# An attention and ternary-FFN layer on eight cores: weight thresholds one cut earlier, sums eight units ahead, the causal mask added on VectorE, and one query product for 129 rows

## The reference, cut to what matters

```python
# x: (2, 16384, 1024), 16 heads of 64, 4 sinks, window 512, FFN 1024 -> 4096 -> 1024
def attn(x):                       # x is the layer-normed input
    q, k, v = split_heads(x @ Wq), split_heads(x @ Wk), split_heads(x @ Wv)
    ctx = 4 sinks + last 512 positions of k and v          # t_ctx = 516
    logits = einsum(q, ctx_k) / 8
    logits = where(cols <= rows + (516 - t), logits, -inf) # so only the last
    w = softmax(logits); w = where(isnan(w), 0, w)         # 516 rows see anything
    return einsum(w, ctx_v) @ Wo
def bitlinear(x, W):
    scale = clip(mean(abs(W), axis=1), 1e-5)
    return x @ (clip(round(W / scale), -1, 1) * scale).T
def ffn(x):
    h = bitlinear(x, w_fc) + gate * (x @ v.T @ fast_b.T @ u.T)
    return bitlinear(relu(h) ** 2, w_proj)
x = x + layernorm(attn(layernorm(x)))
x = x + layernorm(ffn(layernorm(x)))
```

## Time and profile before

| | us |
|---|---|
| three runs | 1111.68 (median), 1111.23, 1113.1 |
| the profiled execution | 1114.61 |
| its span, slowest core (core 5) | 1113.0 |
| spans of the eight cores | 1104.3 to 1113.0 |
| PE busy | 1036.8 (93%) |
| DVE busy | 577.4 (52%) |
| ACT busy | 372.6 (33%) |

### The profile page before, as it was taken

How to read it: one execution, slowest core, us unless ns; L and a number is a source line. 1 busy time by engine, 2 the same in 40 slices (tenths; PEclk the granted TensorE clock), 3 DMA queues, 4 the chain that set the end, 5 groups by cost and what they waited for, 6 DMA issues and landing times.

```text
span 1113.0 us, 15478 instructions; the slowest of 8 cores (1104.3 to 1113.0 us)
## 1 busy us (share of the span) xinstructions
PE 1036.8 (93%) x5173; PEld 477.1 (43%) x5173; DVE 577.4 (52%) x905; ACT 372.6 (33%) x701; POOL 15.7 (1%) x33
## 2 busy tenths in 40 slices
PE   3788858977999999999999999999999999999997
PEld 1222335533454444444445444454444444444443
DVE  3878889676343553454434353454435544444333
ACT  4577798313431143112421044112421143014300
POOL 0000000000000000000000000000000000000000
PEclk9988967998999999999999999999999999999999
DMA  8999976474123511362043510572016310321011
GB/s 261 202 228 231 225 248 210 117 202 137 36 54 93 144 44 23 87 149 70 19 63 93 142 44 6 98 159 94 16 29 150 107 39 6 102 84 39 1 61 54
DMA packets 101489, 115.91 MB, mean 104 GB/s; under 512 B 77581, under 2 KB 77837, under 8 KB 101412
## 3 DMA queue, kind: packets, MB, share of 16 engines
q1 hardware_dynamic: 97444, 102.59, 34.6%
q0 software_dynamic: 3728, 12.25, 5.9%
q10 hardware_dynamic: 240, 0.07, 0.0%
HBM read 87.79 MB, written 17.31 MB: 94 GB/s over the span
## 4 chain that ended last, share of the span: by engine, by line
PE 86%; DVE 5%; issue 4%; DMA 2%; ACT 2%; DVEq 0%; ACTq 0%; SPq 0%; POOLq 0%
PE fcb L477 38%; PE pjp L491 36%; PE xp L491 1%; PE xp L531 1%; PE xp L628 1%; PE xp L590 1%; PE fcb L491 1%; DVE below L1196 1%; PE pjp L542 1%; DMA r<-v 1%; DVE below L1202 1%; DMA lrow<-ctx 1%; DMA xy<-wpj 1%; PE xp L670 0%; PE xp L613 0%
## 5 line engine op out<-in xcount | busy, mean ns | idle before, releaser
L477 PE MATMUL fcb<-xnT,Sfc 128*128 128x512 bf16 x2048 | 468.2, 388 | 4.8 <-DVE r L1144 4.7
L491 PE MATMUL pjp<-Spj,r 128*128 128x512 fp8e4 x1920 | 422.5, 380 | 0.0
L477 PEld LDWEIGHTS fcb<-xnT,Sfc 128*128 128x128 bf16 x2048 | 198.9, 99 | 257.6 <-issue 36.1
L491 PEld LDWEIGHTS pjp<-Spj,r 128*128 128x128 bf16 x1920 | 185.9, 98 | 223.9 <-issue 5.7
L1144 DVE TENSOR_TENSOR r<-fcb,rpp 128x512 bf16<-128x512 f32 x224 | 154.3, 691 | 236.2 <-ACT rpp L841 235.1
L841 ACT ACTIVATE rpp<-fcb,hsc 128x512 f32<-128x512 f32 x224 | 153.6, 687 | 238.2 <-PE fcb L477 237.5
L813 ACT ACTIVATE lv<-mv,cvecs 128x1 f32<-128x1 f32 x64 | 18.7, 293 | 304.4 <-DVE mv L1126 216.8
L1116 DVE TENSOR_TENSOR xy<-pjp,oscb 128x512 f32<-128x512 f32 x60 | 41.3, 688 | 151.1 <-PE pjp L491 151.1
L1121 DVE BATCH_NORM_STATS2 s<-xy 128x6 f32<-128x512 f32 x64 | 44.4, 694 | 9.1 <-DVE xy L1116 5.7
L1138 DVE TENSOR_TENSOR xy<-xy 128x1024 f32<-128x1024 f32 x32 | 39.1, 1223 | 4.7 <-DVE xy L1130 4.7
L542 PE MATMUL pjp<-identb,tern 128*128 128x128 bf16 x256 | 25.2, 257 | 15.3 <-DVE tern L1206 8.5
(11 more groups left out here) (138 smaller groups left out, 529.9 us busy)
## 6 DMA issues: line engine op xcount, KB each, us to landing
out<-xy SPq DMA_DIRECT2D x32, 512.0 KB, 2.9
xy<-x SPq DMA_DIRECT2D x31, 512.0 KB, 4.9
xs<-x SPq DMA_DIRECT2D x29, 512.0 KB, 4.9
xy<-wfc SPq DMA_DIRECT2D x16, 512.0 KB, 5.0
xy<-wpj SPq DMA_DIRECT2D x13, 512.0 KB, 5.2
stg<-wpj SPq DMA_DIRECT2D x11, 512.0 KB, 5.1
stg<-wfc SPq DMA_DIRECT2D x10, 512.0 KB, 5.3
xs<-wpj SPq DMA_DIRECT2D x8, 512.0 KB, 5.1
```

The costliest lines, as they stand in the source:

```text
L477: mm = te.matmul(fcb[n % 3][:, 0:TT], s_fc[:, dci * HF + hc * 128:dci * HF + hc * 128 + 128], xnT[:, dci * TT:(dci + 1) * TT], start=(dci ...
L491: mm = te.matmul(dst, r2[:, hc * TT + s * 128:hc * TT + s * 128 + 128], s_pj[:, hc * D + half * 512: hc * D + half * 512 + 512], start=(hc ...
```

## The change

- `AHEAD` is 8 instead of 7: ACT does the sum of unit n + 8 in step n, and one sum more before the loop.
- `group` of the fc units (but the first) stands ahead of `cut(n + 2)`, not behind it. `ut` moves from steps n % 4 == 1, ahead of `fc`, to steps n % 4 == 0, behind `fc`. `ut_copy` moves to the end of steps n % 4 == 0. The first such group keeps its place (n == 0 and n == 1).
- The mask has 516 columns, zero for the sinks, and is added by DVE: `Sm` = `xp` + `mask`; maximum and exponential read `Sm`. PE no longer multiplies it in.
- `queries` multiplies the 128 rows and the lone row at once, 129 columns.

```diff
--- before.py
+++ after.py
@@ -38,7 +38,7 @@
 NUNIT = NFU + NPU
 GRP = 4
 NSLOT = 9
-AHEAD = 7
+AHEAD = 8
 
 NG = 6
 GROWS = [128, 128, 128, 128, 128, 5]
@@ -69,7 +69,7 @@
     DI = lambda n, s: nc.dram_tensor(n, s, F32, kind="ExternalInput")
     t_x = DI("x", [TOK, D])
     t_ctx = DI("ctx", [CN, D])
-    t_mw = DI("mw", [128, WIN])
+    t_mw = DI("mw", [128, CTX])
     t_ms = DI("ms", [NH, SINKS])
     t_cvec = DI("cvec", [128, 8])
     t_id = DI("ident", [128, 128])
@@ -135,7 +135,8 @@
             QB = asb("QB", [128, DCN * NH], BF16)
             KS = asb("KS", [128, DCN * SINKS], BF16)
             VS = asb("VS", [SINKS, D], BF16)
-            mask = asb("mask", [128, WIN], BF16)
+            mask = asb("mask", [128, CTX], BF16)
+            Sm = asb("Sm", [128, CTX], F32)
             msB = asb("msB", [NH, SINKS], F32)
             OT = asb("OT", [128, DCN * NACT + 2], BF16)
             ast6 = asb("ast6", [128, 12], F32)
@@ -607,15 +608,14 @@
             def queries(q):
                 w = wt(3 * q + 1)
                 te.wait_ge(a_k, 2 * q + 2)
-                for lo, n, at in ((CA, 128, 0), (CB, 1, 256)):
-                    for kk in range(2):
-                        for dc in range(DCN):
-                            mm = te.matmul(
-                                xh[0][:, at + kk * n:at + kk * n + n],
-                                w[:, dc * 256 + kk * 128:
-                                  dc * 256 + kk * 128 + 128],
-                                ctxT3[:, dc, lo:lo + n],
-                                start=(dc == 0), stop=(dc == DCN - 1))
+                for kk in range(2):
+                    for dc in range(DCN):
+                        mm = te.matmul(
+                            xh[0][:, kk * NACT:kk * NACT + NACT],
+                            w[:, dc * 256 + kk * 128:
+                              dc * 256 + kk * 128 + 128],
+                            ctxT3[:, dc, CA:CA + NACT],
+                            start=(dc == 0), stop=(dc == DCN - 1))
                 mm.then_inc(p_q, 1)
 
             def values(q, k):
@@ -643,8 +643,6 @@
                 q, k = divmod(h, 4)
                 r = slice(64 * (h % 2), 64 * (h % 2) + 64)
                 te.wait_ge(a_q, q + 1)
-                if h == 0:
-                    te.wait_ge(d_msk, 32)
                 if k > 0:
                     te.wait_ge(a_e, h)
                 if k == 1:
@@ -652,10 +650,9 @@
                 if k == 2:
                     te.wait_ge(a_o, 2 * q + 1)
                 qa = QA[r, (k // 2) * 128:(k // 2) * 128 + 128]
-                te.matmul(xh[0], identb[:], mask[:], start=True, stop=False)
                 te.matmul(xh[0], qa, KT[r, (k // 2) * WIN:
                                         (k // 2) * WIN + WIN],
-                          start=False, stop=True)
+                          start=True, stop=True)
                 te.matmul(xh[1][:, 0:SINKS], qa,
                           KS[r, (h // 2) * 4:(h // 2) * 4 + 4],
                           start=True, stop=True).then_inc(p_s, 1)
@@ -761,12 +758,12 @@
             for n in range(NUNIT):
                 if n >= NFU:
                     unit(n)
-                if n % GRP == 1 and n + 3 < NFU:
-                    ut(n // GRP + 1)
                 if 2 <= n < HCN + 2:
                     fc(0, n - 2)
                 if n == 0:
                     low_rank(2)
+                if n == 1 or (n > 1 and n % GRP == 0 and n + 4 < NFU):
+                    ut(n // GRP + 1)
                 if n + 3 < NFU:
                     low_rank(n + 3)
                 if n > NFU and n % GRP == 3:
@@ -905,12 +902,15 @@
                 sc.wait_ge(p_q, q + 1)
                 if q == 0:
                     sc.wait_ge(v_zero, 1)
-                sc.activation(QA[:], xh[0][:, 0:256], AF.Copy)
+                sc.activation(QA[:].rearrange("p (k n) -> p k n", n=128),
+                              xh[0][:, 0:2 * NACT].rearrange(
+                                  "p (k n) -> p k n", n=NACT)[:, :, 0:128],
+                              AF.Copy)
                 for e in range(2):
                     r = slice(64 * e, 64 * e + 64)
                     at = 36 * q + e
                     cp = sc.activation(QB[r, at:at + 19:18],
-                                       xh[0][r, 256:258], AF.Copy)
+                                       xh[0][r, 128:2 * NACT:NACT], AF.Copy)
                 cp.then_inc(a_q, 1)
 
             def values(q, k):
@@ -926,7 +926,7 @@
                 sc.wait_ge(v_mx, h + 1)
                 if h > 0:
                     sc.wait_ge(d_pt, 16 * h)
-                sc.activation(Pb[:, 0:CTX], xp[:, 0:CTX], AF.Exp, scale=0.125,
+                sc.activation(Pb[:, 0:CTX], Sm[:], AF.Exp, scale=0.125,
                               bias=nmx[:, 1:2],
                               accum_out=nmx[:, 2:3]).then_inc(a_e, 1)
 
@@ -1023,18 +1023,21 @@
             turned(3)
             abssum(5)
             abssum(6)
+            abssum(7)
             for n in range(NUNIT):
                 if n + AHEAD < NUNIT:
                     abssum(n + AHEAD)
                 if n >= NFU:
                     evac(n)
-                if n % GRP == 1 and n + 3 < NFU:
-                    ut_copy(n // GRP + 1)
+                if n == 1:
+                    ut_copy(1)
                 if n == NFU + 15:
                     out_scale(0)
                 if 3 <= n < HCN + 3:
                     relu(0, n - 3)
                     square(n - 3)
+                if n > 1 and n % GRP == 0 and n + 4 < NFU:
+                    ut_copy(n // GRP + 1)
             out_scale(1)
             for j in range(NTILE):
                 i = NSUB * j
@@ -1232,8 +1235,12 @@
                                  ALU.mult).then_inc(v_lnr, 1)
 
             def scores(h):
+                if h == 0:
+                    ve.wait_ge(d_msk, 32)
                 ve.wait_ge(p_s, h + 1)
-                settled(ve.reduce_max(nmx[:, 0:1], xp[:, 0:CTX], axis=AX.X,
+                settled(ve.tensor_tensor(Sm[:], xp[:, 0:CTX], mask[:],
+                                         ALU.add))
+                settled(ve.reduce_max(nmx[:, 0:1], Sm[:], axis=AX.X,
                                       negate=True))
                 ve.tensor_scalar(nmx[:, 1:2], nmx[:, 0:1], 0.125, None,
                                  ALU.mult).then_inc(v_mx, 1)
@@ -1297,10 +1304,12 @@
             cut(0)
             cut(1)
             for n in range(NUNIT):
+                if n > 1 and n % GRP == 0 and n + 4 < NFU:
+                    group(n // GRP + 1)
                 if n + 2 < NUNIT:
                     cut(n + 2)
-                if n % GRP == 0 and n + 4 < NFU:
-                    group(n // GRP + 1)
+                if n == 0:
+                    group(1)
             for j in range(NTILE):
                 i = NSUB * j
                 more = j + 1 < NTILE
@@ -1383,7 +1392,9 @@
             [x[beta, T - WIN:T], act, one, x[beta, 0:SINKS]], axis=0))
         jw = np.arange(WIN)[None, :]
         rr = 128 * i + np.arange(128)[:, None]
-        m["mw"] = np.where(jw <= rr, 0.0, NEG).astype(np.float32)
+        m["mw"] = np.concatenate(
+            [np.where(jw <= rr, 0.0, NEG), np.zeros((128, SINKS))],
+            axis=1).astype(np.float32)
         cs = np.arange(SINKS)[None, :]
         m["ms"] = np.ascontiguousarray(np.broadcast_to(
             np.where(cs <= i, 0.0, NEG).astype(np.float32), (NH, SINKS)))
```

## The result

The changed kernel took **1105.54 us** (median of 4 runs, 1103.62 to 1106.7), the kernel before 1112.39 beside it (4 runs, 1111.23 to 1113.9). The ratio is 0.9936, 95% interval 0.9916 to 0.9956: 6.85 us less, where 10.3 were forecast. The profiled execution took 1105.06 us; its slowest core is core 2. Some executions of every kernel, changed or not, show a lower granted clock on part of the cores and take longer; all ratios here leave these out.

What follows compares the result with a forecast made beforehand. PE was taken as full in the tiles, a DVE-PE-ACT wait loop as limiting the fc units. Terms -9.7 + 2.0 + 1.2 - 3.5 - 1.5 + 1.2 = -10.3 us, from 1111.68 to 1101.4 us; range 1095 to 1108.5.

Steps and rivals of the forecast that it cites:

- parts 1 and 2: Fc units: thresholds first in the step remove a loop of waits, -9.7 us; loads landing late then cost +2.0.
- part 1: Fc units: thresholds one cut earlier leave no wait in the DVE-PE-ACT loop, 12.1 us a group, -9.7 us.
- the group that was to hide: Fc units: the second group of thresholds hides in DVE's wait ahead of unit 6, put at 0.7 us.
- part 3: Projection units: unit 47's copy on ACT waits behind a sum whose load is asked for later, +1.2 us, bounds 0 and 2.1.
- part 4: Attention: 16 mask matmuls leave PE, 0.216 us each, -3.5 us; 5.0 if the change of weights costs more.
- part 5: Attention queries: 16 matmuls a call instead of 32, four calls at 0.38 us, -1.5 us.
- part 6: Attention: mask add on DVE delays exponential, relus and squares, so PE waits at seven fc-stage scores, +1.2 us, bounds 0 and 5.6.
- the loads': Fc units: landings near 7 us keep the spacing nearly as before, 1107.5 us; chance 0.2.
- the clock's: Fc units: the granted clock still falls once a group, 0.5 us a group leaks through, 1104.4 us; chance 0.1.
- the slower one: Fc units: the turn's new place lowers the clock longer in every group, 15.01 us spacing, 1116.2 us; chance 0.04.
- The mask rival: Attention: the mask add stalls PE at every score, costing 5.6 us for 1.2, 1105.8 us; chance 0.06.

Runs made afterwards that it cites:

- copy first: Changed kernel, but in projection units ACT does the unit's copy first, then relu and square, the sum last: ratio to the kernel before 0.9897, again 0.9893.

## Why the prediction was right, and where it was off

On the mean core the time to the first projection group fell by 7.6 us, the projection units gave 4.3 back (80.5 for 76.2 from that group to their end), and 2.9 came off the rest: 6.2 us less. The prediction had -7.7 (parts 1 and 2), +1.2 and -3.8. So 3.1 us of what it missed are the projection units and 0.9 the attention; that the first number agrees is chance, as its two terms were off by nearly the same, each the other way.

**Thresholds first, and loads (parts 1 and 2).** Right in mechanism: from the fourth group on the wait for the low-rank product is gone from the loop, which takes 11.9 us a group at clock 1.00 where no load is late. That is four times 2.7 and 1.1, which make 11.9 and not the 12.1 that the prediction says, so its 1.2 us for the difference were not needed. The loads cost less than 2.0: they held the thresholds for 0 to 1.7 us a core, 0.6 on the mean one. That leaves 8.2 us for part 1, where it had 9.7. Two things that the sum left out lie behind the difference; they are not priced apart. It was made on core 5, the slowest of the kernel before (first group at 134.4, the mean 132.9), where the same step took off 10.6 us. And on three cores (2, 4 and 6) the group that was to hide did not, and the spacing from 45 us on was 14.5 us, with a wait of 1.86 for the low-rank product at 51.51 on core 2. Its fc products and window there:

```profile
45.10:59.60 14.50, 14.45 (x52) 4.60 (x52) 11.16 (x18) 8.63 (x15) 0.00 (x0) 1.00 0.82 187
```
```profile
47.11 3.59 PE L478 MATMUL fcb<-xnT,Sfc 128*128 128x512 bf16 x8
...
51.55 1.90 PE L478 MATMUL fcb<-xnT,Sfc 128*128 128x512 bf16 x8
```

Eight products took 3.59 us there, the pace of the lower level, and 1.90 from 51.55 on. The other five cores had 1.90 from 43 us on. The window reads 1.00 nonetheless: this core's first record of the clock in the kept trace is the rise at 50.8 us, and a stretch ahead of the first record reads 1.00 whatever the clock was. What held the clock down 8 us longer on these cores was not looked into. The reported time is that of the slowest core, now core 2.

**Projection units (part 3) is the step that failed in size,** +1.2 for +4.3. The prediction named the right queue: the copy stands behind the next load's sum, whose load is asked for one cut later. It priced this at the copy of unit 47 alone, and capped it at one cut, 2.1 us. But it begins at unit 32. There too the copy now stands behind the sum of one unit more, 40 for 39, with the wait for its load (1.43 us on core 2, 2.54 with eight ahead alone) and the sum itself (1.06), and comes 3.4 us later on the mean core. After that ACT takes 3.25 us a unit while relus and squares last, then 1.94, and is the engine PE waits for (16.6 us in place of 6.8 on core 2), so it can't make them up: at that pace the 15 steps from unit 32's copy to unit 47's take 33.0 us, and they took 33.9 before, so no more than 0.9 were there to win. They took 35.0 in the changed kernel, as more sums ahead of copies wait for their loads there (on core 2 0.33, 0.40 and 0.56 us from 160 to 168 us, for 0.25 once before). All kernels in which the copy stands behind no such sum (seven ahead in the projection units, seven ahead throughout, copy first) have the loss gone, and the kernel before with nothing but the lead of eight has it whole.

**Mask (part 4) and queries (part 5)** came to 0.22 a score, -3.5, and 0.39 a call, -1.6, as worked out. The change of weights costs nothing that shows: 0.22 is the pitch alone.

**Mask add on DVE (part 6)** cost 1.8 to 1.9, not 1.2. The chain was right, mask add, exponential, relu, square, bank, and doubling the add moved every gap by its length. I had given five of the seven scores 0.1 us; all seven stall for 0.27. Of that 0.09 is the exponential, which I took as 0.06 shorter when it reads SBUF, by a relu and a square as the rows at hand. It got 0.03 longer (725 ns for 691). The Trainium skill, "VectorE: DVE Perf Modes", section on the TRN2 errata, had the direction and nearly the size (0.04); an instruction of another form was the worse guide. The other 0.08 of the 0.17 us a score stays open.

**The signs.** The prediction calls itself wrong if the spacing stays at 13.6, which it did not, or if the tiles with attention are not each about 1 us shorter. That sign came, at half strength: the second to fourth are 0.98, 0.83 and 0.67 us shorter on the mean core, and the last, which holds two scores, is 0.05 longer (122.50 for 122.44). With 0.22 won at a score and 0.27 lost where it stands in an fc stage, a tile gains by its scores in projection stages and by its queries only.

**The load estimate from the Trainium skill** ("DMA: Bandwidth & Descriptors"), 2.5 us for a unit's two transfers and so nothing lost, was nearer to the 0 to 1.7 us measured (0.6 on the mean core) than my 2.0. A spacing of 12.00 us, four units, holds at 276 GB/s:

```profile
71.70:83.70 12.00, 10.25 (x44) 3.67 (x43) 11.20 (x17) 9.52 (x18) 0.00 (x0) 1.00 1.17 276
```

(Core 2 of the changed kernel, columns of the earlier trace rows.) Of the rivals, the loads', the clock's and the slower one didn't come: on all cores the granted clock reads 1.00 in every window of 12 us from 44 to 128 us, but for one at 0.86 (on the three cores above it counts from 51 us only). The mask rival had the right number of stalls, 0.27 us each where it had 0.8; with two adds they were 1.07. That 1105.5 lies near some of their times is chance.

## What to carry to other kernels

When work is asked for earlier, look at everything that stands behind it in its own queue, at the first place where it matters and not at the last: a queue with no slack keeps a delay that it has once taken. A change of several parts should be priced with each part undone, since one here (eight units ahead) cost over half of what another gained and wasn't needed by it. And work moved to an idle engine is free only where the instruction queued behind it is nobody's release; often a swap with its neighbour makes it so.

## What was unexpected of the hardware

The maximum over 128x516 took 691 ns from SBUF (L1243), and 681 from PSUM before the change: reading SBUF did not make it shorter. The attention is repeated to a hundredth of a microsecond: four tiles, from the second with attention on, have the same mean length in both profiled runs of the changed kernel (124.29, 123.87, 123.96, 122.50 us). Where the cores' clocks agree, the spread between cores and runs lies in the units and the tiles ahead of these, so an edit to the tiles can be priced from one trace far below the 0.2% of a timing.
